# Extra PE products between the first value projection and the second batch's projections of a transformer block

## The chip, the cores and the metric

The kernel runs on one core of one Trainium2 chip. The metric is the device time of one execution in microseconds (us). PE is TensorE, DVE is VectorE, ACT is ScalarE, POOL is GpSimd and SP is SyncE; PEld is PE's weight load.

## The reference, cut to what matters

One pre-norm transformer block on x of shape (4, 512, 128): attention with 16 heads of size 8, ALiBi slopes and a causal mask, and then an FFN with all 8 experts (hidden size 256), whose sum is scaled by a gate.

```
x = x + attn(layernorm(x))     # qkv = x @ w_attn + b; scores = q k / sqrt(8) + slope * pos, causal; softmax; @ v; @ w_proj + b
x = x + ffn(layernorm(x))      # h = gelu(x @ w1[e] + b1[e]); y[e] = h @ w2[e] + b2[e]; sum over e of y[e], times norm_g
```

norm_g is g / (g + 1e-6) with g the largest softmax gate of the RMS-normed logits.

## The kernel before

Each engine has its queue written out by hand in one function; counting semaphores tie them together. The work goes by batch b (4 of them) and, within a batch, by set s (4 sets of 4 heads, "quads"). A projection of a batch (`project_qk`, `project_v`) needs the transposed normalised x (`transpose_x` on PE, `take_xT` on DVE, which splits it into a high and a low part so that products in a fast form keep their accuracy).

For every set the maxima of the scores are needed before the exponentials. In `max_unit` PE computes a block of scores into one of three banks (`v_ring`), and DVE reduces it with the mask to a row maximum (L1189). A set has eleven such units. PE can be three banks ahead: a unit waits until DVE has freed the bank of the unit three before it. Behind the eleventh unit, `transpose_max` turns the maxima on PE, `take_max` on DVE negates and splits them, and DMAs of SP (and once ACT) put them into `q_stack` as further rows, so that the exponent's score product (`exp_unit`, banks `a_ring`) already has the maximum subtracted.

The start is laid out like this on PE: 18 products of ones (`idle_products(18)`, L992: a tile `unused` set to 1.0 against itself, written to `ffn_bank`, which nobody reads at that point), the transposition of batch 0, 3 more products of ones, the projections K, Q and V of batch 0, the transposition of batch 1 (L998), the eleven maximum units of set 0 and `transpose_max`, the projections K, Q and V of batch 1, the first maximum units of set 1, and then the long loop, in which a plan says at which of 16 places of a set each maximum unit, exponent unit and product with V stands. In that loop the first set's plan puts six maximum units of set 1 ahead and then alternates one maximum unit and one exponent unit.

On DVE the same stretch is: statistics and normalisation of batch 0, its split, statistics of batch 1 (`take_x(1)`), K and Q of batch 0 (`first_parts`), V of batch 0, the inverse root for batch 1 (`root_x(1)`, eleven tiny steps, each waited for), `normalise_x(1)`, the split of batch 1, the maximum units of set 0, `take_max`, K, Q and V of batch 1, the maximum units of set 1. PE's `transpose_x(1)` waits for `xn_ready`, which `normalise_x(1)` raises.

`ident_bf` is a 128 x 128 identity in bf16 that POOL writes near the start (L554); the same instruction raises `mask_ready` to 1. `ffn_bank` is next written by the FFN (L933), whose first product of a batch starts the accumulation anew.

Of the kernel before, what the change touches and what calls it, by code (L numbers as in the profile page):

```python
# [35 lines left out]
P = 128  # L36
# [70 lines left out]
def block_kernel(nc, x, w_attn, w_proj, w1, w2, columns, rows, consts, out):  # L107
# [5 lines left out]
    TB = T // P  # L113
# [18 lines left out]
    with ExitStack() as ctx:  # L132
        def sb(name, shape, dt=F32):
            return ctx.enter_context(nc.sbuf_tensor(name, shape, dt))

        def bank(name):
            return ctx.enter_context(nc.psum_tensor(name, [P, 512], F32))

        def sem(name):
            return ctx.enter_context(nc.semaphore(name))  # L140
# [5 lines left out]
        ident_bf = sb("ident_bf", [P, P], BF16)  # L146
# [91 lines left out]
        ffn_bank = bank("ffn_bank")  # L238
# [28 lines left out]
        mask_ready = sem("mask_ready")  # L267
# [44 lines left out]
        def q_count(b):  # L312

            return Q_LOADS * (b + SETS - 2 if b else 0) + 16 * max(0, b - 2)
# [416 lines left out]
        def _(pe):  # L731
# [3 lines left out]
            def v_bank():  # L735

                n = uses[0]
                uses[0] += 1
                if n >= V_BANKS:
                    pe.wait_ge(v_freed, n - V_BANKS + 1)  # L740
                return v_ring[n % V_BANKS]
# [10 lines left out]
            def split_product(dst, lhs, rhs):  # L752

                pe.matmul(dst, lhs[0], rhs[0], start=True, stop=False)  # L754
                pe.matmul(dst, lhs[0], rhs[1], start=False, stop=False)  # L755
                return pe.matmul(dst, lhs[1], rhs[0], start=False, stop=True)  # L756


            def idle_products(count):

                for _ in range(count):
                    pe.matmul(ffn_bank[:], unused[:, 0, 0:P], unused[:, 0, :], start=True, stop=True)

            def transpose_x(b):
                pe.wait_ge(xn_ready, b + 1)
                if b == 0:
                    pe.wait_ge(ident_set, 1)
                dst = v_bank()
                for n in range(TB):
                    last = pe.transpose(dst[:, n * P:(n + 1) * P], xn[:, n, :], ident)  # L770
                last.then_inc(v_filled, 1)

            def project_qk(b, part):
                pe.wait_ge(xT_ready, b + 1)
                if b == 0:
                    pe.wait_ge(wa_split, 2)
                cols = slice(part * C, (part + 1) * C)
                dst = v_bank()
                split_product(dst[:], (w_attn_hi[:, cols], w_attn_lo[:, cols]),
                              (xT_hi[:], xT_lo[:])).then_inc(v_filled, 1)  # L780

            def project_v(b):
                cols = slice(2 * C, 3 * C)
                dst = v_bank()
                for n in range(TB):
                    tok = slice(n * P, (n + 1) * P)
                    last = split_product(dst[:, tok], (xT_hi[:, tok], xT_lo[:, tok]),
                                         (w_attn_hi[:, cols], w_attn_lo[:, cols]))
                last.then_inc(v_filled, 1)


            def max_unit(b, s, k):
                if k == 0 and b < 2 and s == 0:
                    pe.wait_ge(q_const, SETS * (b + 1))
                if k == 0 and b == 0 and s % 2 == 0:
                    pe.wait_ge(k_const, QUADS * (s // 2 + 1))
                if k == 0 and b == 0 and s == 0:
                    pe.wait_ge(first_q_loaded, Q_LOADS)
                elif k == 0 and b == 0 and s < SETS - 1:
                    pe.wait_ge(q_loaded, Q_LOADS * (SETS - 2))  # L800
                elif k == 0:
                    pe.wait_ge(q_loaded, q_count(b + 1))
                n, quads = MAX_UNITS[k]
                if n == TB - 1 and s % 2 == 0:
                    pe.wait_ge(k_loaded[s // 2][quads[0]], K_LOADS * (b + 1))
                    pe.wait_ge(k_low_loaded[s // 2][quads[0]], K_LOW_LOADS * (b + 1))
                cols = P * (n + 1)
                dst = v_bank()[:, 0:len(quads) * cols].rearrange("p (q t) -> p q t", t=cols)
                pe.matmul(dst, q_stack[b % 2][:, s, n * P:(n + 1) * P],  # L809
                          k_stack[:, s, quads[0]:quads[-1] + 1, 0:cols], start=True, stop=True).then_inc(v_filled, 1)  # L810

            def transpose_max(b, s):
                n = SETS * b + s
                pe.wait_ge(max_ready, n + 1)
                dst = v_bank()
                pe.transpose(dst[0:TB * QUADS, 0:P], row_max[:, n % 2, :], ident).then_inc(v_filled, 1)  # L816
# [141 lines left out]
            def side(b, s, k):  # L958

                for stage, of in due(STAGES, b, s, k, B):  # L960
                    if stage == "y_low":
                        transpose_y(of, 0)
                    if stage == "y_high":
                        transpose_y(of, 1)
                    if stage == "y_norm":
                        transpose_y_norm(of)
                    if stage == "attention":
                        project_y(of)
                    if stage == "z":
                        transpose_z(of)  # L970
                    if stage == "logits":
                        logits(of)
                    if stage == "ffn":
                        transpose_ffn(of)
                    if stage == "x":
                        transpose_x(of)
                    if stage == "q":
                        project_qk(of, 0)
                    if stage == "k":
                        project_qk(of, 1)  # L980
                    if stage == "v":
                        project_v(of)
# [8 lines left out]
            pe.wait_ge(warm_set, 1)  # L991
            idle_products(18)  # L992
            transpose_x(0)
            idle_products(3)
            project_qk(0, 1)
            project_qk(0, 0)
            project_v(0)
            transpose_x(1)  # L998
            for k in range(len(MAX_UNITS)):
                max_unit(0, 0, k)  # L1000
            transpose_max(0, 0)
            project_qk(1, 1)
            project_qk(1, 0)
# [444 lines left out]
```

## Time and profile before

| | |
|---|---|
| median of 3 runs | 312.45 us (312.29 to 312.54) |
| the profiled execution | 311.52 us |
| its span on the core | 309.8 us |
| mean granted PE clock, share of full | 0.963 |
| PE busy | 283.4 us, 91% of the span |
| DVE busy | 206.7 us, 67% |
| ACT busy | 187.2 us, 60% |
| POOL busy | 90.3 us, 29% |

Times in rows are microseconds from the start of the span unless they are marked ns. PE's clock has two levels, 2.4 GHz (granted 1.00) and 1.2 GHz (0.50). The durations of PE's products overlap: a product's row is longer than the step to the next one. "<-" in square brackets names what ended the idle time before a row.

### The profile page before, as it was taken

Reading aid. Unit: us, or ns where it says so; the run is one execution under the profiler, and the core shown is the slowest. Engines: PE = TensorE matmul, PEld = TensorE weight load, DVE = VectorE, ACT = ScalarE, POOL = GpSimd, SP = SyncE. Lnnn points to the kernel's source line nnn. Section 1 sums busy time; section 2 is a strip of 40 time slices with the busy share of each in tenths; the row PEclk is TensorE's granted clock in tenths of the full one; section 3 lists DMA queues with packets and bytes.
Section 4 is the critical chain, followed back from the end, with each engine's and each line's share of the span. In section 5 each row is a group of like instructions: output and inputs, shape, how many; then the busy total and the mean of one; then the engine's idle time right before and its main releaser. Section 6 shows DMA issues by size and latency. Waiting matters only on the chain.

```text
span 309.8 us, 5270 instructions
## 1 busy us (share of the span) xinstructions
PE 283.4 (91%) x1643; PEld 181.9 (59%) x1643; DVE 206.7 (67%) x831; ACT 187.2 (60%) x290; POOL 90.3 (29%) x212
## 2 busy tenths in 40 slices
PE   8527899999779999999999999999999999989993
PEld 3413665655547666757566576666566655647871
DVE  5878668787877767565777784648776821367871
ACT  6480066746539376958467296857397796525462
POOL 1449200713133246021431164020400333500250
PEclk9955789999999999999999999999999999999998
DMA  7441005230300023004000141011001000000101
GB/s 203 160 121 45 4 2 201 51 112 17 108 2 2 0 55 115 0 8 114 0 6 0 38 120 44 2 41 47 3 2 38 0 3 2 0 1 2 34 0 34
DMA packets 12811, 13.47 MB, mean 43 GB/s; under 512 B 2224, under 2 KB 9264, under 8 KB 12528
## 3 DMA queue, kind: packets, MB, share of 16 engines
q1 hardware_dynamic: 11596, 11.89, 12.4%
q0 software_dynamic: 1024, 1.05, 1.6%
q8 instruction: 13, 0.21, 0.3%
q10 hardware_dynamic: 164, 0.21, 0.3%
q14 instruction: 14, 0.11, 0.1%
HBM read 5.40 MB, written 1.05 MB: 21 GB/s over the span
## 4 chain that ended last, share of the span: by engine, by line
PE 61%; DVE 25%; POOL 5%; issue 4%; ACT 2%; DMA 1%; DVEq 0%; POOLq 0%; ACTq 0%
DVE unused L1189 14%; PE ffn_bank L933 11%; PE pv_bank L865 8%; PE v_ring L809 8%; PE a_ring L831 8%; PE a_ring L754 5%; PE a_ring L755 4%; PE a_ring L756 4%; PE a_ring L843 3%; POOL var L375 1%; PE v_ring L816 1%; DVE z L1087 1%; PE v_ring L894 1%; PE v_ring L878 1%; POOL var L376 1%
## 5 line engine op out<-in xcount | busy, mean ns | idle before, releaser
L1189 DVE CUSTOM_DVE_ANT_0 unused<-v_ring,cst 128x256 bf16<-128x256 f32 (+3 forms) x256 | 111.4, 488 | 44.2 <-PE v_ring L809 39.8
L620 ACT ACTIVATE probs<-a_ring 128x512 f32<-128x512 f32 x160 | 86.9, 599 | 70.2 <-PE a_ring L843 40.9
L809 PE MATMUL v_ring<-k_stack,q_stack 128*128 128x512 f32 (+1 forms) x176 | 82.2, 506 | 3.6 <-DVE row_max L1189 1.8
L831 PE MATMUL a_ring<-q_stack,k_stack 128*128 128x512 f32 (+3 forms) x256 | 63.3, 329 | 0.3 <-ACT probs L620 0.3
L638 ACT ACTIVATE hidden<-a_ring,cols_sb 128x512 f32<-128x512 f32 x64 | 43.1, 689 | 27.8 <-PE a_ring L756 27.7
L831 PEld LDWEIGHTS a_ring<-q_stack,k_stack 128*128 128x128 f32 x256 | 45.1, 192 | 13.3 <-issue 5.5
L933 PE MATMUL ffn_bank<-hidden,w_sb 128*128 128x512 f32 x100 | 51.4, 599 | 0.9 <-ACT hidden L638 0.9
L809 PEld LDWEIGHTS v_ring<-k_stack,q_stack 128*128 128x128 f32 x176 | 34.1, 200 | 25.4 <-issue 11.4
L865 PE MATMUL pv_bank<-probs,v_ones 128*32 128x256 f32 (+3 forms) x512 | 42.4, 440 | 0.0
L539 POOL TENSOR_SCALAR_AFFINE_SELECT probs<-probs 128x512 f32<-128x512 f32 x16 | 10.1, 634 | 105.9 <-ACT probs L620 105.9
L754 PE MATMUL a_ring<-zT_hi,w_hi 128*128 128x512 f32 x64 | 28.2, 441 | 0.8 <-DVEq L1073 0.8
L843 PE MATMUL a_ring<-score_mask,ident_bf 128*128 128x256 bf16 x96 | 27.2, 283 | 0.0
L755 PE MATMUL a_ring<-zT_lo,w_hi 128*128 128x512 f32 x64 | 25.2, 394 | 0.0
L756 PE MATMUL a_ring<-zT_hi,w_lo 128*128 128x512 f32 x64 | 25.1, 392 | 0.0
L351 POOL DMA_DIRECT2D k_stack<-k_lo x32 | 18.1, 569 | 21.4 <-PE a_ring L843 15.6
L1189 DVE DVE_READ_ACCUMULATOR2_ANT row_max<- 128x1 f32 x256 | 21.4, 84 | 0.0
L865 PEld LDWEIGHTS pv_bank<-probs,v_ones 128*32 128x32 f32 x512 | 12.3, 108 | 15.5 <-issue 13.2
L933 PEld LDWEIGHTS ffn_bank<-hidden,w_sb 128*128 128x128 f32 x100 | 16.9, 192 | 4.3 <-ACT hidden L638 2.3
L754 PEld LDWEIGHTS a_ring<-zT_hi,w_hi 128*128 128x128 f32 x64 | 12.0, 188 | 9.2 <-issue 4.4
L638 ACT ACT_TABLE_LOAD x13 | 16.7, 1283 | 0.2
L620 ACT ACT_TABLE_LOAD x11 | 14.1, 1283 | 0.2
L756 PEld LDWEIGHTS a_ring<-zT_hi,w_lo 128*128 128x128 f32 x64 | 12.0, 188 | 2.8
(130 smaller groups left out, 340.6 us busy)
## 6 DMA issues: line engine op xcount, KB each, us to landing
k_stack<-k_hi SPq DMA_DIRECT2D x60, 32.0 KB
q_stack<-q_hi SPq DMA_DIRECT2D x6, 256.0 KB
hidden<-w SPq DMA_DIRECT2D x1, 1024.0 KB, 7.5
k_stack<-k_lo POOLq DMA_DIRECT2D x32, 32.0 KB, 2.1
x_res<-x SPq DMA_DIRECT2D x4, 256.0 KB, 2.8
w_sb<-w SPq DMA_DIRECT2D x1, 1024.0 KB, 7.1
out<-result SPq DMA_DIRECT2D x4, 256.0 KB, 2.2
x_in<-x SPq DMA_DIRECT2D x3, 256.0 KB, 3.1
```

The lines of the kernel that those rows point to most:

```text
L351: queue.dma_start(k_stack[ROW_Q * q + g::ROW_D, 2 * half:2 * half + 2, q, :].bitcast(F32), part[rows:rows + QR // 2, :].bitcast(F32)).then ...
L620: act.activation(probs[:, n % 2, quads[0]:quads[-1] + 1, KIND_AT[kind]:KIND_AT[kind] + cols], a_bank()[:, 0:len(quads) * cols].rearrange(" ...
L638: act.activation(hidden[:, n % HB, :], a_bank()[:], ACT.Gelu, bias=b1_cols[:, m:m + 1]).then_inc(g_freed, 1)
L754: pe.matmul(dst, lhs[0], rhs[0], start=True, stop=False)
L755: pe.matmul(dst, lhs[0], rhs[1], start=False, stop=False)
L756: return pe.matmul(dst, lhs[1], rhs[0], start=False, stop=True)
L809: pe.matmul(dst, q_stack[b % 2][:, s, n * P:(n + 1) * P], k_stack[:, s, quads[0]:quads[-1] + 1, 0:cols], start=True, stop=True).then_inc(v ...
L831: last = pe.matmul(dst[:, at:at + P * (TB - j)], k_stack[:, s, q, j * P:(j + 1) * P], q_stack[b % 2][:, s, j * P:T], start=(at == 0), stop ...
L843: pe.matmul(diagonal, ident_bf[:], score_mask[:].unsqueeze(1).to_broadcast([P, blocks, P]), start=False, stop=True, skip_group_check=True) ...
L865: last = pe.matmul(pv_bank[QR * q:QR * (q + 1), j * P:T], v_ones[b % 2][:, j, s, q, :], probs[:, n % 2, q, at:at + cols], start=(s % 2 == ...
L933: pe.matmul(ffn_bank[:], w2_sb[:, m, :], hidden[:, n % HB, :], start=(m == 0), stop=(m == NT - 1)).then_inc(ffn2_done, 1)
L1189: ins = dve.tensor_tensor_reduce(unused[:, (uses[0] - 1) % V_BANKS, at:at + cols], bank_[:, at:at + cols], cst[:, C_MASK + T - cols:C_MASK ...
```

## The change

Behind the value projection of batch 0, PE runs 26 products of ones. Behind the transposition of batch 1 it waits for `mask_ready` at 1 and runs three "idle units"; a unit is one product of the identity with the identity broadcast four times, 512 columns in bf16, into `ffn_bank`. One unit stands behind each of the eleven maximum units of set 0, and three more in front of `transpose_max`. Nothing else changes: no result depends on these products.

```diff
+            def idle_units(count):
+
+                for _ in range(count):
+                    pe.matmul(ffn_bank[:], ident_bf[:], ident_bf[:].unsqueeze(1).to_broadcast([P, TB, P]),
+                              start=True, stop=True)
...
             project_v(0)
+            idle_products(26)
             transpose_x(1)
+            pe.wait_ge(mask_ready, 1)
+            idle_units(3)
             for k in range(len(MAX_UNITS)):
                 max_unit(0, 0, k)
+                idle_units(1)
+            idle_units(3)
             transpose_max(0, 0)
             project_qk(1, 1)
             project_qk(1, 0)
```

## Rows read from the trace of the kernel before

**Rows 1.** The page: PE's busy time, and granted clock in 40 slices.

```profile
PE 283.4 (91%) x1643; PEld 181.9 (59%) x1643; DVE 206.7 (67%) x831; ACT 187.2 (60%) x290; POOL 90.3 (29%) x212
...
PEclk9955789999999999999999999999999999999998
```

**Rows 2.** Table by stage: length, busy us (instructions) of each engine, clock, DMA.

```profile
core 0: us, PE busy (x) PEld busy (x) DVE busy (x) ACT busy (x) POOL busy (x), PEclk, DMA share, GB/s
...
13.80:17.00 3.20, 0.00 (x0) 0.00 (x0) 2.77 (x7) 0.10 (x1) 2.42 (x4) 1.00 0.39 97
17.00:20.80 3.80, 0.01 (x1) 0.01 (x1) 2.92 (x15) 3.80 (x4) 0.00 (x0) 0.50 0.43 126
...
30.50:34.00 3.50, 3.49 (x11) 2.92 (x12) 1.76 (x4) 0.00 (x0) 2.43 (x3) 0.50 0.02 5
34.00:37.40 3.40, 2.40 (x14) 1.57 (x13) 2.26 (x8) 0.00 (x0) 0.00 (x0) 0.99 0.00 0
37.40:40.80 3.40, 3.36 (x9) 2.35 (x9) 3.40 (x15) 0.75 (x2) 0.00 (x0) 0.51 0.02 5
...
44.00:48.00 4.00, 4.00 (x43) 1.81 (x41) 0.45 (x2) 2.11 (x4) 0.00 (x0) 1.00 0.10 37
...
81.80:85.20 3.40, 2.17 (x17) 1.77 (x16) 3.12 (x16) 1.68 (x3) 0.96 (x4) 1.00 0.58 166
```

**Rows 3.** The chain of waits, 20 to 37 us: start, us, what.

```profile
20.79 1.13 PE v_ring L770 x4
...
23.73 0.69 DVE unused L1189
...
24.91 0.60 DVE unused L1189
25.52 0.47 DVE unused L1189
...
31.80 0.43 PE v_ring L756
...
36.32 0.69 DVE unused L1189
```

**Rows 4.** Timeline of PE: start, us, instruction, idle time before it.

```profile
8.53 0.65 PE L770 MATMUL v_ring<-cst,xn 128*128 128x128 f32 x4 [0.40 <-DVE xn L1087]
9.02 0.81 PE L762 MATMUL ffn_bank<-unused 128*128 128x512 bf16 x3
...
12.12 0.40 PE L756 MATMUL v_ring<-xT_hi,w_attn_lo 128*128 128x512 f32 x1
12.35 0.22 PE L754 MATMUL v_ring<-w_attn_hi,xT_hi 128*128 128x128 f32 x1
...
13.53 0.27 PE L756 MATMUL v_ring<-w_attn_hi,xT_lo 128*128 128x128 f32 x1
20.79 1.11 PE L770 MATMUL v_ring<-cst,xn 128*128 128x128 f32 x4 [6.99 <-DVE xn L1087]
...
30.51 0.38 PE L816 MATMUL v_ring<-cst,row_max 128*16 128x128 f32 x1 [1.27 <-DVEq L1197]
...
43.20 0.28 PE L816 MATMUL v_ring<-cst,row_max 128*16 128x128 f32 x1 [0.59 <-DVEq L1197]
...
89.80 0.66 PE L902 MATMUL v_ring<-cst,z 128*128 128x128 f32 x4 [1.56 <-DVE z L1087]
```

**Rows 5.** Timeline of DVE, the same columns.

```profile
9.22 0.69 DVE L1070 CAST xT_hi<-v_ring 128x512 fp32r<-128x512 f32 x1 [0.28 <-PE v_ring L770]
...
21.94 0.69 DVE L1070 CAST xT_hi<-v_ring 128x512 fp32r<-128x512 f32 x1 [1.21 <-PE v_ring L770]
...
35.15 0.88 DVE L1175 TENSOR_TENSOR v_ones<-v_ring,rows_sb 128x128 f32<-128x128 f32 x4 [0.85 <-PE v_ring L756]
...
43.51 0.28 DVE L1205 TENSOR_SCALAR m_hi<-v_ring 16x128 fp32r<-16x128 f32 x1 [0.43 <-PE v_ring L816]
```

**Rows 6.** Timelines of POOL and of ACT's queue, and q's time to landing.

```profile
1.81 0.29 POOL L554 TENSOR_SCALAR_AFFINE_SELECT ident_bf<-zeros 128x128 bf16<-128x128 f32 x1
...
16.27 0.58 ACTq L361 DMA_DIRECT2D q_stack<-q_lo  x1
...
q_stack<-q_lo ACTq DMA_DIRECT2D x1, 64.0 KB, 3.1
```

## Prediction

> **What bounds the kernel now.** I read the page's busy line first: PE is busy 91% of the span. The line of granted clock under it shows where that is not work at full speed: below nine in slices 3 to 6 of 40, and nowhere else [rows 1]. The table by stage cuts that piece finely [rows 2]. From 13.8 us PE has nothing to do (0.00 of 3.20 busy) at full clock (2.4 GHz); from 17.0 the clock is at half (1.2 GHz). It is still at half from 30.5 to 34.0, where PE is busy 3.49 of 3.50 us. It is full from 34.0, half again from 37.4 to 40.8, behind a stretch with pauses (2.40 of 3.40 busy), and then full.
>
> The chain of waits says who sets the pace there [rows 3]. PE's transpositions of the second batch's x are on it (20.79), then the split of their result on DVE. Then DVE's own queue is decisive: its first maximum block begins at 23.73 and its pieces follow one another without a gap, 0.61 us apart for 512 columns (24.91 to 25.52) and 0.47 for 384; PE is ahead by the ring of three banks. At 30.5 PE is late again: DVE waits for the transposed maxima and for each projection, the last time 0.85 us for V at 35.15 [rows 5]. The second block starts on DVE at 36.32 [rows 3] and again runs without a gap, while PE stands 0.59 us in front of its transposition at 43.20 [rows 4]. From 44.0 PE is busy without a break, 4.00 of 4.00 [rows 2]. So the path is DVE and PE's short pieces until 43.2 us, and PE from there on. What is taken out ahead of 43.2 starts the PE-bound rest that much earlier.
>
> **The 26 products.** They stand behind the value projection, whose last product starts at 13.53 [rows 4]; with its 0.11 us step they begin at 13.64. Three such products at full clock span 0.81 us [rows 4]; with 0.40 for the last one's length that is a step of (0.81 - 0.40) / 2 = 0.205, and the projection's 512-column products step 0.23 (12.12 to 12.35 [rows 4]). I take 0.22. 26 x 0.22 = 5.7 us, so they end at 19.35, and 1.44 us are left until the normalised x is there at 20.79. Their cover is PE's idle 6.99 us in front of that row [rows 4]. They read a tile that was set at the start and write the FFN's bank, which nobody reads yet. Without the cover each costs 0.22 us, at half clock 0.43 (a projection piece there [rows 3]). The Trainium skill, "TensorE: Matmul & The Clock Gate", section "Back-to-back issue gap", gives about 131 ns for a 512-column product in a real stream; by that the 26 would last 3.4 us, end at 17.0 and leave 3.7 us of pause, with more room for the clock to fall. The rows say 0.2 and more, and the trace decides.
>
> **The transposition of the second batch.** At half clock DVE is idle 1.21 us until PE has done it (21.94 [rows 5]). At full clock, for the first batch, the four instructions take 0.65 us from 8.53 [rows 4] and DVE's next row starts at 9.22 [rows 5]: 0.69 behind the start of the first. In the second batch it is 21.94 - 20.79 = 1.15. Gain 1.15 - 0.69 = **0.46 us**, if the clock is still full 1.4 us behind the last product.
>
> **The wait on the mask, and 3 + 11 + 3 idle units.** The wait is for an identity that POOL has written by 2.10 us [rows 6]: nothing. A unit is one product of 512 columns, 0.22 us. The first three, 0.66 us, go from about 21.3 to 21.95 and delay the first maximum product; DVE wants that only behind its split rows, at 23.73 - 0.46 = 23.27. Cover 1.0 us or more. Its inputs have landed by then: the low part of q is issued at 16.27 and takes 3.1 us [rows 6]. The 11 single units stand between maximum products. At full clock a pair is 0.23 + 0.22 = 0.45 us or less against DVE's 0.61 and 0.47, with two banks of lead: nothing on the path, though with 0.02 us to spare on the 384 ones. At half, a 512 pair is 0.86 and a 384 pair 0.32 + 0.43 = 0.75, together 1.61 against DVE's 1.08: PE would be late by 0.26 a unit, less its lead. The last three (0.66) lie in PE's idle 1.27 us in front of the transposition of the maxima at 30.51 [rows 4]. What all of them do is shorten PE's pauses in a block in which the clock was half.
>
> **Transposed maxima and projections of batch two.** I count from the start T of the transposition of the maxima. Before, T = 30.51 [rows 4] and DVE starts on V at 35.15 [rows 5], T + 4.64. At full clock DVE starts on the maxima at T + 0.31 (43.20 [rows 4] to 43.51 [rows 5]) and has them some 0.6 later. K is three 512 products from T + 0.10: its end is T + 0.10 + 2 x 0.23 + 0.40 = T + 0.96. DVE takes K from T + 1.0 and Q from T + 1.85. V starts on PE at T + 0.10 + 6 x 0.23 = T + 1.5; in batch one its twelve products began at 12.35 and ended at 13.53 + 0.27 = 13.80 [rows 4], 1.45 us. So it ends at T + 2.95 and DVE starts on it at **T + 3.0**. Gain 4.64 - 3.0 = **1.64 us**.
>
> **The second block and after.** DVE starts it 0.46 + 1.64 = 2.10 us earlier, at 34.22, and would end at 41.0. No idle units stand in it, so I expect the half stretch of 37.4 to 40.8 again. At 37.4 PE then has three maximum and four or five score products left before the next transposition of maxima; put one behind the other at half clock, with the banks as DVE frees them, they end at 41.1 to 41.2. So 0 to 0.2 of the gain is lost at PE, whose slack of 0.59 is used up. I take 0.05. Behind 44 us everything is released by PE, DVE or loads that follow from the maxima, and moves with them. **Sum: 2.10 - 0.05 = 2.05 us.** The profiled span of 309.8 (its run 311.52) becomes 307.75 (309.5). The median of the runs shown is 312.45, 0.93 above the profiled run; the same gain makes **310.4**.
>
> **The rivals.** All hang on the clock.
> (a) *A late half stretch.* From 81.8 to 85.2 us PE is busy 2.17 of 3.40, and at 89.80 it has waited 1.56 for z, and the clock held [rows 2, 4]; from 34.0 to 37.4 it was busy 2.40 of 3.40 and the clock fell. So work of the kind of 82 to 90 us, coming 2 us earlier, may meet a fall that it just missed. Price: a half stretch as long as that of 37.4 to 40.8 over PE-bound work costs 3.4 / 2 = 1.7 us. Gain 0.35, 312.1.
> (b) *The idle units are not enough*, and the clock falls inside or at the end of the first maximum block. For it: the fall at 37.4; and a pause of about 0.9 us stays behind the last units. If it falls in the middle, PE paces the block for some 3.4 us: 3.4 x (1 - 1.08 / 1.61) = 1.1, less two banks' lead of 1.1, so 0 to 1.1 lost. If at the end, the projections go at half again and mostly the 0.46 stays, with 0.1 from the maxima's transposition. Gain 0.6 to 2.0, middle 1.1: 311.3. The same page of the Trainium skill, section on the PE-mode transpose, says that transposes do not bring the full clock; by that this case would begin at the x transposition. The trace has no stretch of transposes alone that would tell.
> (c) *The 26 products go at half.* Then they last 26 x 0.43 = 11.2 us and end at 24.8, 4.0 us behind 20.79; with 2.05 gained later that is 1.95 slower, 314.4. Each product at half adds 0.21, so it decides from 1.44 / 0.21 = 7 of them on, and makes the kernel slower than before once about 17 are. Against it: the clock is full until 17.0 even with PE empty [rows 2].
> (d) *Slower, by a fall at the end of the first block*: then the rest moves by only 0.6 us, and meets the late fall of (a) with that. 0.6 gained, 1.7 lost: 313.5. It decides once what is gained ahead of 43.2 is below 1.7.
> (e) *More than the sum*: the 0.93 us by which the median exceeds the profiled run may be part of a late half stretch in those runs, which the new placing avoids: 2.05 + 1.7 = 3.75, 308.7.
>
> **How the numbers follow.** Forecast 0.52 (310.4, by itself 309.8 to 310.9); (a) 0.13; (b) 0.18; (c) 0.02; (d) 0.05; (e) 0.10. About 0.2% (0.6 us) can be told from no change, so faster is below 311.8. Faster: 0.52 + 0.10 + 0.14 of (b) + 0.02 of (a) = 0.78. Same: 0.04 of (b) + 0.11 of (a) = 0.15. Slower: (c) and (d), 0.07. The range leaves out (c), (d) and (e), 0.17: 309.7 to 312.3.
>
> **What would show it.** Granted clock 1.00 from 13.6 to at least 33 us; the x transposition about 0.65 us long at 20.8; in the first block pairs of 0.45 us on PE and DVE's rows unbroken from 23.27 to 29.9; DVE's V row at about 33.05 and its second block at 34.2; PE's transposition of the second maxima at about 41.15. Wrong would be: clock 0.50 anywhere from 14 to 33, a gap of DVE inside the first block, the x transposition later than 20.8, or a half stretch between 60 and 300 us.

## The result

The changed kernel takes 309.74 us (median of 5 runs, 309.52 to 310.13) against 312.45 (5 runs, 311.70 to 312.64): a ratio of 0.9921 with a 95% interval of 0.9905 to 0.9937, 2.7 us faster. The forecast was 310.4 in a range of 309.7 to 312.3, so the median lies only just inside the range, and 0.7 below the forecast. The profiled run has a span of 307.7 us (before: 309.8) and a time of 309.52; the forecast for these was 307.75 and 309.5.

Over all sets of runs of this study the two medians are 310.02 (23 runs) and 312.40 (98 runs), 2.4 us apart.

| | before | after |
|---|---|---|
| span | 309.8 | 307.7 |
| mean granted PE clock | 0.963 | 1.000 |
| PE busy | 283.4 | 288.0 |
| DVE busy | 206.7 | 206.4 |
| ACT busy | 187.2 | 187.5 |

The page's line of granted clock, which had two fives, a seven and an eight in slices 3 to 6 in [rows 1], is now:

```profile
PEclk9999999999999999999999999999999999999999
```

The table by stage of the profile after (length, busy us and instructions of each engine, clock, DMA) answers to [rows 2]. PE is busy where it was idle or in pieces, and the clock is full in each row:

```profile
13.60:17.00 3.40, 3.35 (x17) 1.54 (x17) 2.79 (x8) 0.27 (x1) 2.57 (x4) 1.00 0.34 80
17.00:20.80 3.80, 2.53 (x13) 1.07 (x12) 2.91 (x15) 3.80 (x4) 0.07 (x1) 1.00 0.43 138
...
30.10:33.50 3.40, 3.38 (x21) 2.69 (x20) 2.32 (x6) 0.00 (x0) 2.67 (x3) 1.00 0.02 5
33.50:37.40 3.90, 2.59 (x6) 1.04 (x6) 3.62 (x17) 0.00 (x0) 0.00 (x0) 1.00 0.00 0
37.40:40.80 3.40, 2.92 (x13) 1.79 (x13) 3.40 (x19) 3.08 (x6) 0.63 (x1) 1.00 0.00 0
```

PE's timeline after, from the 26 products on (one of their records is missing), answers to [rows 4]:

```profile
13.56 5.79 PE L762 MATMUL ffn_bank<-unused 128*128 128x512 bf16 x25
20.62 0.66 PE L776 MATMUL v_ring<-cst,xn 128*128 128x128 f32 x4 [1.27 <-DVE xn L1098]
21.11 0.81 PE L767 MATMUL ffn_bank<-ident_bf 128*128 128x512 bf16 x3
21.57 0.58 PE L815 MATMUL v_ring<-k_stack,q_stack 128*128 128x512 f32 x1
...
27.81 0.50 PE L815 MATMUL v_ring<-k_stack,q_stack 128*128 128x512 f32 x1
28.15 1.04 PE L767 MATMUL ffn_bank<-ident_bf 128*128 128x512 bf16 x4
29.88 0.28 PE L822 MATMUL v_ring<-cst,row_max 128*16 128x128 f32 x1 [0.69 <-DVEq L1208]
...
41.18 0.28 PE L822 MATMUL v_ring<-cst,row_max 128*16 128x128 f32 x1 [0.85 <-DVEq L1208]
```

DVE's timeline after answers to [rows 5]:

```profile
21.31 0.69 DVE L1081 CAST xT_hi<-v_ring 128x512 fp32r<-128x512 f32 x1 [0.75 <-PE v_ring L776]
...
23.10 0.69 DVE L1200 CUSTOM_DVE_ANT_0 unused<-v_ring,cst 128x512 bf16<-128x512 f32 x1 [0.37 <-DVE xT_lo L1082]
...
31.11 0.75 DVE L1172 TENSOR_SCALAR k_full<-v_ring,cols_sb 128x512 f32<-128x512 f32 x1 [0.32 <-PE v_ring L756]
32.17 0.75 DVE L1142 TENSOR_SCALAR q_full<-v_ring,cols_sb 128x512 f32<-128x512 f32 x1 [0.32 <-DVE k_full L1172]
33.24 0.89 DVE L1186 TENSOR_TENSOR v_ones<-v_ring,rows_sb 128x128 f32<-128x128 f32 x4 [0.31 <-PE v_ring L815]
34.40 0.69 DVE L1200 CUSTOM_DVE_ANT_0 unused<-v_ring,cst 128x512 bf16<-128x512 f32 x1 [0.28 <-DVE v_ones L1186]
```

Between the two profiles the 2.0 us up to the second transposition of maxima (43.20 to 41.18) split like this: 0.17 because x was there earlier in this run (20.79 to 20.62), which I put down to chance, as in the other two profiles of the changed kernel it is there at 20.90 and 21.26; 0.46 at the x transposition; 0 in the first block (23.73 to 30.51 and 23.10 to 29.88, both 6.78); 1.28 in the projections (V on DVE 4.64 and now 3.36 behind the maxima's transposition); 0.10 in the second block (36.32 to 43.20, 6.88, and 34.40 to 41.18, 6.78). Behind it nothing changes: 309.8 - 43.2 = 266.6, and 307.7 - 41.2 = 266.5.

### The profile page after: what moved, and what is told of

Same layout as the page of the kernel before. It is cut to its first block, busy times and chain, and to the rows that moved or that the text cites. A ratio compares the mean times of both kernels' runs of the same rounds, so it can differ in the third digit from the quotient of the medians.

```text
span 307.7 us, 5355 instructions
## 1 busy us (share of the span) xinstructions
PE 288.0 (94%) x1685; PEld 182.0 (59%) x1686; DVE 206.4 (67%) x831; ACT 187.5 (61%) x290; POOL 90.2 (29%) x212
## 4 chain that ended last, share of the span: by engine, by line
PE 61%; DVE 25%; POOL 5%; issue 4%; ACT 2%; DMA 1%; DVEq 0%; POOLq 0%; ACTq 0%
DVE unused L1200 14%; PE ffn_bank L939 11%; PE pv_bank L871 8%; PE v_ring L815 8%; PE a_ring L837 8%; PE a_ring L754 5%; PE a_ring L755 4%; PE a_ring L756 4%; PE a_ring L849 3%; POOL var L375 1%; DVE z L1098 1%; PE v_ring L822 1%; PE v_ring L900 1%; PE v_ring L884 1%; POOL var L376 1%
## 5 line engine op out<-in xcount | busy, mean ns | idle before, releaser
L815 PE MATMUL v_ring<-k_stack,q_stack 128*128 128x512 f32 (+1 forms) x176 | 80.6, 489 | 3.1 <-DVE row_max L1200 1.8
L638 ACT ACTIVATE hidden<-a_ring,cols_sb 128x512 f32<-128x512 f32 x64 | 43.2, 690 | 27.7 <-PE a_ring L756 27.6
L815 PEld LDWEIGHTS v_ring<-k_stack,q_stack 128*128 128x128 f32 x176 | 32.4, 190 | 24.6 <-DVE row_max L1200 10.1
L849 PE MATMUL a_ring<-score_mask,ident_bf 128*128 128x256 bf16 x96 | 27.2, 283 | 0.0
L762 PE MATMUL ffn_bank<-unused 128*128 128x512 bf16 x46 | 13.3, 451 | 1.6 <-DVE unused L1345 1.5
```

Of the source, the lines that this page charges most:

```text
L638: act.activation(hidden[:, n % HB, :], a_bank()[:], ACT.Gelu, bias=b1_cols[:, m:m + 1]).then_inc(g_freed, 1)
L815: pe.matmul(dst, q_stack[b % 2][:, s, n * P:(n + 1) * P], k_stack[:, s, quads[0]:quads[-1] + 1, 0:cols], start=True, stop=True).then_inc(v ...
L849: pe.matmul(diagonal, ident_bf[:], score_mask[:].unsqueeze(1).to_broadcast([P, blocks, P]), start=False, stop=True, skip_group_check=True) ...
```

## Experiments

Each kernel ran beside the kernel before on the same chip; the ratios are to it. The chip is not the same in all experiments: the kernel before has medians of 312.55, 312.34 and 312.41 in the three sets, so medians of different sets can be compared to about 0.2 us.

**The kernel before again**, unchanged.

> The kernel before, unchanged, so that span and granted clock of each of its runs are seen. Theory (the gain of 2.7 us between medians is 2.0 us of clock held through the first block and projections, as in the two profiles, and the rest is half stretches that vary from run to run and are mostly longer in the kernel before than in its profiled run): the runs spread over about 1 us, from 311.5 to 312.6, and the longer ones have the lower mean clock (0.963 in the 311.5 one, about 0.955 or less in the 312.5 ones). Rival (the 0.9 us between profiled run and median has nothing to do with the clock): all runs have a mean clock within 0.001 of 0.963 whatever their time.

Median 312.02 (12 runs), beside 35 more at 312.55; ratio 0.9996 (0.9970 to 1.0021). The spread is real, and a large part of it goes with the clock. Of the 93 runs of the kernel before in the experiments, 40 have a mean granted clock of 0.961 or more and a median of 311.62, and 53 have less and a median of 312.65. (The clock is not all of it: the 28 runs with exactly 0.963 lie from 311.09 to 312.44.) The first profile is of the shorter kind. This one (span 310.7, clock 0.958) is of the longer. In its table by stage the clock is half not only until 34.0 but until 42.0:

```profile
18.00:34.00 16.00, 10.99 (x27) 6.95 (x28) 12.09 (x48) 5.40 (x7) 11.32 (x11) 0.51 0.19 55
34.00:42.00 8.00, 7.68 (x22) 5.39 (x22) 6.01 (x24) 1.19 (x2) 0.00 (x0) 0.50 0.01 2
```

DVE's timeline there shows where it is paid. V comes at 35.80 after a wait of 1.70 us where [rows 5] has 0.85:

```profile
23.53 0.69 DVE L1189 CUSTOM_DVE_ANT_0 unused<-v_ring,cst 128x512 bf16<-128x512 f32 x1 [0.37 <-DVE xT_lo L1071]
...
35.80 0.88 DVE L1175 TENSOR_TENSOR v_ones<-v_ring,rows_sb 128x128 f32<-128x128 f32 x4 [1.70 <-PE v_ring L756]
36.97 0.69 DVE L1189 CUSTOM_DVE_ANT_0 unused<-v_ring,cst 128x512 bf16<-128x512 f32 x1 [0.29 <-DVE v_ones L1175]
```

From the first block's start to the second's it takes 36.97 - 23.53 = 13.44 us, against 12.59 in the first profile and 11.30 after. These 0.85 us are most of the 0.93 by which the median of before stands above its profiled run. The rival, the same mean clock in all runs, is refuted. One limit stays: only a run of clock 0.958 was profiled, and 34 of the 53 runs have 0.951 to 0.954. What their clock does is in no profile.

**The 26 products alone.**

```diff
             idle_products(26)
             transpose_x(1)
-            pe.wait_ge(mask_ready, 1)
-            idle_units(3)
             for k in range(len(MAX_UNITS)):
                 max_unit(0, 0, k)
-                idle_units(1)
-            idle_units(3)
```

> The 26 products alone, no idle units and no wait on the mask. Theory (both parts are needed; the products bring the clock as far as the x transposition, the units keep it through the maximum block): x transposition 0.65 us long, then the clock falls inside or behind the first block, the projections K, Q, V go at half; span about 0.5 to 0.7 below before, 309.2, median near 311.8. Rival (the products alone keep it, the units do nothing): span 307.7 and median 309.7, as with both.

Median 311.32, ratio 0.9969 (0.9948 to 0.9990). The x transposition is short (0.66 us at 20.79, DVE's wait 0.75). Then the clock is half from 22.6 to 32.9, through the maximum block, K and Q:

```profile
13.60:20.80 7.20, 5.67 (x27) 2.40 (x27) 5.88 (x23) 3.90 (x4) 2.64 (x4) 1.00 0.39 110
...
22.60:32.80 10.20, 8.19 (x16) 4.82 (x17) 8.28 (x36) 1.01 (x2) 9.98 (x9) 0.50 0.20 47
```

From block to block it takes 35.52 - 23.27 = 12.25 us, 0.34 less than before and 0.95 more than with the units. 7 of the 12 runs lie from 310.55 to 311.48, the other 5 from 312.05 to 312.87 with a lower clock (0.969 or 0.970 instead of 0.973 or 0.974), so a longer half stretch, as in the kernel before, may still be there in some; none of these five was profiled. The products alone give the 0.46 and some of the rest: the median gain of 1.2 is more than the 0.5 to 0.7 expected, in the profile by the 0.34 (the clock is back at 32.9 and not at 34.0) and 0.10 in the second block.

**The idle units alone.**

```diff
             project_v(0)
-            idle_products(26)
             transpose_x(1)
```

> The idle units alone, without the 26 products. Theory: the clock falls at about 17 and the x transposition takes 1.1 us as before; in the block PE is busy without a pause at half (pairs of 0.86 and 0.75 us against DVE's 0.61 and 0.47), so the block's end on DVE is up to 1 us late, but the clock comes back in the block and the projections go at full: DVE's V row 1.3 us closer to the maxima's transposition. Gain 1.3 minus 0 to 1.0 plus 0: span 308.5 to 309.8, median 310.8 to 312.2. Rival (the products alone make the gain): no gain at all or a loss of 1 us, 313.4.

Median 310.81, ratio 0.9961 (0.9942 to 0.9979). The profile (span 309.3) has what the theory expected. The x transposition takes 1.12 us. The pairs go at half and PE paces DVE, and then the clock is full from 26.5 through the projections, and half once more from 36.7 to 40.1, where the second block takes 6.78 us (35.83 to 42.61) as after. PE's timeline in the block:

```profile
23.22 0.65 PE L767 MATMUL ffn_bank<-ident_bf 128*128 128x512 bf16 x1
23.31 0.88 PE L815 MATMUL v_ring<-k_stack,q_stack 128*128 128x384 f32 x1
23.99 0.65 PE L767 MATMUL ffn_bank<-ident_bf 128*128 128x512 bf16 x1
24.08 0.99 PE L815 MATMUL v_ring<-k_stack,q_stack 128*128 128x512 f32 x1
24.87 0.65 PE L767 MATMUL ffn_bank<-ident_bf 128*128 128x512 bf16 x1
```

From idle unit to idle unit it is 0.77 and 0.88 us, where I had put 0.75 and 0.86. DVE waits for PE inside the block, 0.31 us and 0.25 us at a time:

```profile
23.59 0.69 DVE L1199 CUSTOM_DVE_ANT_0 unused<-v_ring,cst 128x512 bf16<-128x512 f32 x1 [0.41 <-PE v_ring L815]
...
25.11 0.69 DVE L1199 CUSTOM_DVE_ANT_0 unused<-v_ring,cst 128x512 bf16<-128x512 f32 x1 [0.31 <-PE v_ring L815]
...
26.70 0.43 DVE L1199 CUSTOM_DVE_ANT_0 unused<-v_ring,cst 128x256 bf16<-128x256 f32 x1 [0.25 <-PE v_ring L815]
```

The maxima's transposition comes 31.30 - 23.59 = 7.71 us behind the block's start instead of 6.78, 0.93 late. V follows 3.37 behind it, at full clock. So the units pay in the projections (1.27) and lose 0.93 in the block: what the products bring in the complete change is the x transposition and, above all, a block that starts at full clock. Between medians the units alone gain more, 1.7 us: none of their 12 runs has a clock below 0.973, so the long half stretch of the kernel before is gone with them too.

**40 products instead of 26.**

> 40 products of ones instead of 26, everything else as in the changed kernel. Theory: each takes 0.22 us at full clock, the 14 more take 3.0 to 3.1 us, of which PE's pause of 1.27 us in front of the x transposition hides its part; that transposition starts 1.75 us later than 20.6, and all behind it: median 309.7 + 1.75 = 311.5. Rival (they fold into time that is not on the path): under 0.5 us later. If the products went at half clock: 4.8 us later.

Median 311.53 against an expected 311.5, ratio 0.9979 (0.9955 to 1.0003); the x transposition starts at 22.32, 1.70 us later than in the profile after, directly behind the products. Three of the 10 runs, from 312.43 to 313.36, have a clock of 0.985 to 0.989. The products are free only as long as they fit PE's pause.

**The changed kernel again.**

> The changed kernel again, to see its spread beside that of before, whose 47 runs lie in two groups: 21 with a mean clock of 0.961 or more (median 311.59) and 26 with 0.958 or less (median 312.69). Theory (the changed kernel never has the long half stretch ahead of 42 us; what is left are half stretches in the second maximum block, worth 0.1 to 0.5 us, and a rare late one worth 1.7 as in three of the ten runs of the 40 products): no two groups, most runs from 309.5 to 310.2 with clocks of 0.99 to 1.00, at most two of twelve near 311.5; median 309.8, 2.7 below the median of before, of which 0.6 is that before falls into its longer stretch more often than not. Rival (the gain is the 2.0 of the two profiles and the rest was chance of five runs): median 310.3 or more.

Median 310.15, ratio 0.9951 (0.9933 to 0.9969). 7 of the 12 runs lie from 309.44 to 310.16, but 5 from 310.99 to 311.80, three of these with a clock of 0.984 or 0.985: more than the two I had allowed. None is as long as the median of before. The profile (time 310.99, but span 308.3, clock 0.994) shows a place that no rival names: the clock is half from 11.0 to 14.5, in the projections of the first batch. DVE waits 0.28 us for K there and runs some 0.5 us late from then on, and x is there at 21.26 instead of 20.62:

```profile
21.26 0.66 PE L776 MATMUL v_ring<-cst,xn 128*128 128x128 f32 x4 [0.20 <-DVE xn L1098]
```

The second transposition of maxima starts at 41.83 instead of 41.18. The 26 products begin only at 15.28 and all but fill the wait.

**Products, and one piece of 5 units at the end of the block.**

```diff
-            idle_units(3)
             for k in range(len(MAX_UNITS)):
                 max_unit(0, 0, k)
-                idle_units(1)
-            idle_units(3)
+            idle_units(5)
             transpose_max(0, 0)
```

> The 26 products, and instead of 3 + 11 + 3 idle units only 5 in one piece in front of the transposition of the maxima. Theory (in the block the clock falls because of PE's pauses between maximum products; a burst at the end can't keep it): the clock is half behind 23 to 27 us, the units run at half at the end, 5 x 0.43 = 2.1 us against a pause of 1.27, so they delay the maxima's transposition by 0.9 us in some runs and bring the clock back only behind it; median 311.3 to 312, no better than the products alone. Rival (any work in front of the projections is enough): median 309.8.

Median 310.73, ratio 0.9954 (0.9937 to 0.9972), better than expected and than the products alone. The clock does fall (half from 22.8 to 33.0) and the piece does hold the maxima up: they are turned 31.42 - 23.97 = 7.45 us behind the block's start, 0.67 late. In both profiles, this one and that of the products alone, the clock comes back at about 33; the difference is in the runs that were not profiled: no run here is above 311.53, where the products alone have five above 312. My reading, which no profile shows, is that the five units, by which PE has no pause from the last maximum product through K, keep the half stretch from lasting until 42. It would be a cure for the long half stretch, not for the short one.

**Six more units, in the second block.**

```diff
                 for unit in maxima_due(-1, k):
                     if unit[1] == 1:
                         max_unit(*unit)
+                        idle_units(1)
```

> The changed kernel and one more idle unit behind each of the six maximum units of set 1 that stand ahead of the loop. Theory: they keep the clock through the second block, where it fell from 37.0 to 40.4 in the 40-product kernel; PE had 0.61 us of slack in front of the next transposition there all the same, so the gain is 0 to 0.3 us in the runs that have that stretch: median 309.6, clock 1.00 in nearly all runs. Rival (the half stretch in the second block is what separates the 309.5 runs from the 310.1 ones): all runs at 309.5. If the six units delay the first score products: 0.3 to 0.5 slower.

Median 309.77 (6 runs, 309.50 to 310.00), ratio 0.9930 (0.9910 to 0.9950), all clocks from 0.996 to 1.000. In the changed kernel 15 of 23 clocks are 0.990 to 0.994. Such a clock doesn't say where the half stretch is (in the one profile of the changed kernel with 0.994 it is at 11.0 us), but that all six clocks here are above speaks for the second block as its place in most runs. What a half stretch in the second block looks like shows in the next kernel's profile.

**Ten more units, at 83 and 88 us.**

```diff
                         side(b, s, k)
+                        if (b, s, k) == (1, 0, 11):
+                            idle_units(4)
...
                     if stage == "z":
+                        if of == 0:
+                            idle_units(6)
                         transpose_z(of)
```

> The changed kernel and 4 idle units in front of the maximum unit that waits 1.20 us at 83.1, and 6 in front of the transposition of z that waits 1.54 us at 87.7. Theory (the rare runs near 311.5 or 1.7 above the others have their half stretch behind 83 to 88 us): none of them is left, median as the changed kernel, within 0.1; the 10 units (2.15 us) fit the two waits of together 2.74. Rival (the long runs come from elsewhere): as many long runs as the changed kernel. If the waits are shorter than the units somewhere: up to 0.3 slower.

Median 309.96 (6 runs, 309.71 to 310.15), ratio 0.9935 (0.9913 to 0.9956), none long. In its profile the clock is half from 36.9 to 40.3, in the second block. DVE's timeline shows the price, which I had put at 0 to 0.2: from 34.67 to 42.22 it takes 7.55 us to the next maxima, against 7.10 after.

```profile
34.67 0.69 DVE L1204 CUSTOM_DVE_ANT_0 unused<-v_ring,cst 128x512 bf16<-128x512 f32 x1 [0.28 <-DVE v_ones L1190]
...
40.17 0.42 DVE L1204 CUSTOM_DVE_ANT_0 unused<-v_ring,cst 128x256 bf16<-128x256 f32 x1 [0.29 <-PE v_ring L815]
...
42.22 0.28 DVE L1220 TENSOR_SCALAR m_hi<-v_ring 16x128 fp32r<-16x128 f32 x1 [0.43 <-PE v_ring L822]
```

PE still has 0.45 us of pause in front of its transposition, so the loss is not there but at the banks: 0.29 of the 0.45 is one wait of DVE.

**A longer pause for z, empty and filled.** Both carry six more POOL steps ahead of z; the second also has 13 idle units on PE in front of that wait.

```diff
                 inverse_sqrt(pool, settle, rstd2[:], ...)
+                if b == 0:
+                    for _ in range(6):
+                        settle(pool.tensor_tensor(var[:, 1, :], var[:, 0, :], var[:, 0, :], ALU.mult))
...
+                        if of == 0:
+                            idle_units(13)
                         transpose_z(of)
```

> The changed kernel with six more tiny steps on POOL (0.28 us each) behind the inverse root for z of the first batch, so that PE waits about 3.2 instead of 1.54 us for z near 88 us. Nothing of the result changes. Theory (a long enough pause there makes the clock fall over PE-bound work, and that is what the runs of the changed kernel near 311.5 have): the clock is half for about 3.4 us behind the pause; wait 1.7 longer and a half stretch worth 1.7: median 309.9 + 3.4 = 313.3. Rival (a half stretch there is hidden): 309.9 + 1.7 = 311.6.

> As the kernel with the slow z, and 13 idle units (13 x 0.22 = 2.8 us) on PE ahead of the wait of about 3.2 us. Theory: the clock stays full, the longer wait stays: 309.9 + 1.7 = 311.6, that is 1.7 us below the one without the units. Rival: the same time as without the units, or more if they outlast the wait.

Medians 313.28 and 311.57, ratios 1.0030 (1.0013 to 1.0047) and 0.9979 (0.9964 to 0.9994); expected were 313.3 and 311.6. The difference of 1.7 us between medians is the price of the late half stretch as near as runs give it; in the two profiles, from z to the first FFN product, it is 93.73 - 89.71 = 4.02 us against 94.58 - 92.15 = 2.43, so 1.6. The tables by stage, first empty, then filled. The first has PE's pause and, behind it, the work at half clock; the second has the units in the pause (z is there at 92.15, since x came late in this execution, the longest of the 12) and no half clock there:

```profile
86.50:89.80 3.30, 0.10 (x2) 0.10 (x2) 1.11 (x4) 2.05 (x3) 1.39 (x7) 1.00 0.02 5
89.90:93.20 3.30, 3.30 (x26) 1.84 (x29) 2.10 (x6) 0.00 (x0) 0.00 (x0) 0.50 0.02 5
```

```profile
86.50:89.80 3.30, 3.09 (x23) 1.45 (x22) 1.90 (x14) 1.75 (x4) 2.33 (x13) 1.00 0.00 0
89.90:93.20 3.30, 2.91 (x19) 1.40 (x21) 1.47 (x5) 1.11 (x1) 0.68 (x4) 1.00 0.02 5
```

**The changed kernel a third time, and with all 16 further units.**

> The changed kernel beside the three others on one chip. Theory: one to five of twelve runs between 311 and 312 with a clock of 0.984 to 0.989, the others from 309.4 to 310.2; median 309.9. Rival (the long runs of the second set were chance of that chip): none above 310.5.

> The changed kernel with the six more units in the second block and the ten around 83 and 88 us. Theory: neither half stretch is left, the clock is 1.00 in all runs; what still varies is when x arrives, some 0.5 us: runs from 309.4 to 310.0, median 309.7, none above 310.5. Rival: runs near 311.5 as in the changed kernel's second set (5 of 12 above 310.9).

The changed kernel: median 309.92, ratio 0.9926 (0.9907 to 0.9946), five of 6 runs from 309.63 to 310.53 and one at 311.75. The profile is of that one (span 310.0), and has rival (a) in it. PE waits 1.53 us for z, works at full clock for a moment, and then at half. (It has a half stretch in the second block too, from 37.9 to 41.3.)

```profile
85.00:88.90 3.90, 2.15 (x19) 1.14 (x12) 2.51 (x14) 2.63 (x4) 1.58 (x8) 1.00 0.01 2
89.10:92.40 3.30, 3.30 (x27) 1.15 (x25) 2.83 (x11) 0.00 (x0) 0.10 (x1) 0.50 0.02 6
92.50:96.00 3.50, 3.50 (x19) 2.91 (x16) 0.96 (x5) 2.48 (x4) 2.44 (x13) 1.00 0.00 0
```

In PE's timelines the 24 products with V take 2.79 us in this run and 1.50 in the profile after:

```profile
88.49 0.66 PE L908 MATMUL v_ring<-cst,z 128*128 128x128 f32 x4 [1.53 <-DVE z L1098]
88.90 0.96 PE L815 MATMUL v_ring<-k_stack,q_stack 128*128 128x512 f32 x2
89.79 2.79 PE L871 MATMUL pv_bank<-probs,v_ones 128*32 128x384 f32 x24
92.51 0.50 PE L754 MATMUL a_ring<-zT_hi,w_hi 128*128 128x512 f32 x1
```

```profile
87.73 0.66 PE L908 MATMUL v_ring<-cst,z 128*128 128x128 f32 x4 [1.54 <-DVE z L1098]
...
88.72 1.50 PE L871 MATMUL pv_bank<-probs,v_ones 128*32 128x384 f32 x24
90.16 0.50 PE L754 MATMUL a_ring<-zT_hi,w_hi 128*128 128x512 f32 x1
```

From z to the first FFN product it is 92.51 - 88.49 = 4.02 us against 2.43: 1.6 us.

With all further units: median 309.74 (4 runs, 309.58 to 309.90), ratio 0.9909 (0.9897 to 0.9922), none long. But the clock is not 1.00 in all, as the theory had it: the four have 0.994 to 0.999, and in the profile (0.994) it is half from 11.2 to 14.6, in the first batch's projections, where no filler stands. It is the best ratio of the study, but its interval overlaps that of the changed kernel. None of the 16 runs of the three kernels with more units (6, 6 and 4) is above 310.15, while 6 of the 23 of the changed kernel are above 310.9, five of them with a clock below 0.990. That speaks for the pauses at 83 to 88 us as the place of the rare long runs; the late stretch was seen in one profile, and that the second-block units alone also had none above 310 in 6 runs shows that so few runs can't settle how often it comes.

## Why the prediction was right, and where it was off

- *The bound, and the rest moving along.* Right: 266.6 and 266.5 us behind the second transposition of maxima.
- *The 26 products.* Forecast 13.64 to 19.35 with 1.44 us to spare; measured 13.56 to 19.35 with 1.27, as x came 0.17 earlier. The step is (5.79 - 0.39) / 25 = 0.216, the missing record's product counted. The Trainium skill, "TensorE: Matmul & The Clock Gate", section "Back-to-back issue gap", gives about 131 ns for such a product in a stream. The trace doesn't agree: 0.216 us. That they cost 0.22 each beyond the pause was shown with 40 of them.
- *The x transposition*: 0.46 forecast, 0.46 measured. The same page of the Trainium skill, section on the PE-mode transpose, has it that transposes don't bring the full clock, by which rival (b) would have begun there. With the products in front and the units behind, the clock was 1.00 there in the profile after; 0.66 us of transposition among other products don't test the sentence.
- *The idle units* are free at full clock, and at half PE paces DVE as forecast: 0 lost in the first block after, 0.93 with the units alone.
- *Projections: the term that was mis-sized.* T is the start of the maxima's transposition. I had V at T + 3.0 and got T + 3.36, a gain of 1.28 and not 1.64. DVE takes K at T + 1.23 and not T + 1.0, and Q 1.06 us behind K, where I had 0.85, and V 1.07 behind Q: 0.75 us of work and 0.31 or 0.32 of idle time in front of each. The prediction names no row for its 0.85; in the first batch DVE's rows stand 0.88 and 0.99 apart. PE's part was right: its V ends at 32.61 + 0.28 = 32.89, T + 3.01 for a forecast T + 2.95. DVE starts on V 0.35 behind that, its own Q having ended at 32.92. So at full clock this piece is bound by DVE, not by PE.
- *The second block.* I expected the half stretch again at a price of 0.05. In the profile after there was none. In five profiles of kernels with the complete change there was one; the time from the first transposition of maxima to the second, 11.30 us after, gives its price:

| kernel | half clock from the block's start on DVE | to the second transposition | price |
|---|---|---|---|
| longer z pause, empty | + 0.6 to + 4.1 | 11.31 | 0.0 |
| 40 products | + 0.9 to + 4.4 | 11.34 | 0.0 |
| ten late units | + 2.2 to + 5.6 | 11.77 | 0.45 |
| longer z pause, filled | + 2.7 to + 6.1 | 11.85 | 0.55 |
| changed kernel, third | + 3.2 to + 6.6 | 11.75 | 0.45 |

  The prediction had it at 37.4 behind a start at 34.22, + 3.2, where it costs 0.45 and not 0.05. The slack of PE in front of its transposition was the wrong place to look, as the delay goes through the ring of banks.
- *The sum.* 2.05 forecast and 2.1 between the two profiles. The 0.36 too much in the projections was made up by 0.17 of x that came earlier, by the second block (0.10 gained where 0.05 was to be lost) and by 0.1 behind it. So the profiled span was hit partly by luck.
- *The median.* 2.7 and 2.4 us instead of 2.05, and 309.74 is 0.04 inside the lower end of the range. That the median of before is 0.93 above its profiled run was carried over to the changed kernel, whose median is only 0.22 above its own (309.74 and 309.52). This is rival (e) in kind: the kernel before has more half clock in 53 of 93 runs than in the profiled one. But in the one such run that was profiled it is not the late stretch that I had named, worth 1.7; it is the early one, lasting until 42 us instead of 34 and worth 0.85. For the 34 runs with a clock still lower it stays open. The change takes the long early stretch away, as no run of the changed kernel has a mean clock below 0.984.
- *Rival (a)* exists, at a place and a price as forecast (88 to 92 us; 1.6 and 1.7 us). One profile shows it; by clock and time at most 5 of the 23 runs can have it.
- *Rival (b)*, a fall inside or at the end of the first block, is in no profile of a kernel with the complete change. What failed once is the condition of the 0.46, a full clock until x is there: in the profile of the kernel with the filled z pause the statistics of the second batch waited 1.78 us for the load of x, PE's pause behind the 26 products was 2.82 us, the clock fell at 22.1, and the x transposition took 1.12 us. The units then brought it back at 25.5, and the block still took 31.99 - 25.21 = 6.78.
- *A fall that no rival names*, ahead of the whole change: half clock from 11 to 14.5 us, in two of the nine profiles of kernels with the complete change (11.0 and 11.2). In the first it made x some 0.5 late.
- *One reading of the page was short.* The last of the 40 slices in [rows 1] is below nine too: the clock is half for the last 2.7 us of the kernel before, in which no engine computes. It costs nothing, but it lowers that run's mean clock by 0.004 (2.7 / 2 / 309.8), so a mean clock is only a rough count of half stretches.
- *(c) and (d)* did not happen in any profile: wherever the products have a row, 26 of them take 5.79 us.

## What to carry to other kernels

Where an engine with a clock that falls in pauses is not the bound for a while, look at what it does at half speed when it is next on the path: that piece is what filler work buys, and it costs nothing only while it fits the pauses at full clock. Count the waits and semaphore steps of the engine that takes over as the bound, not only its instructions. And look at more than one execution before putting a price on a clock stretch: one profile may show its short form.

## What the runs showed of the hardware

- The same kernel has half stretches of different length in different executions: until 42.0 us instead of 34.0 in the kernel before, with the same instructions in front.
- At half clock PE was busy 3.26 of 3.50 us between 23.7 and 27.2 us (maximum products alone, kernel before) and the clock stayed half; with an idle unit behind each PE was busy 3.90 of 3.90 us from 22.5 to 26.4, and the clock was full from 26.5 (units alone).
- The same pauses led to a fall in some executions and not in others. In the kernel before PE paused 0.57 and 0.43 us in front of two maximum products, and the clock fell at 37.4; in the profile after it paused 0.75 and 0.43 there (busy 2.59 of 3.90 us), and the clock held. Near 84 and 88 us the pauses were 1.20 and 1.54 us in the profile after, where it held, and 1.22 and 1.53 in the third, where it fell at 89.1.
- The time at which the normalised x of the second batch is there differs by up to 1.6 us between profiles (the x transposition starts from 20.59 to 22.22 where PE is waiting for it). The largest delays stand behind waits of DVE for the load of x (1.78 us for 22.22, 1.12 us for 21.49), one behind half clock in the first batch's projections (21.26). A fixed number of filler products ahead of such a wait leaves a pause that varies by as much.
